# The first tile of a neighbour-maximum kernel is picked before the rest of its batch is prepared

## What is computed

```
scores = where(adj != 0, -arange(N), -inf)
vals, idx = top_k(scores, 25);  valid = vals > -inf
feats = where(valid[..., None], x[idx], -inf);  agg = feats.max(axis=2)
agg = where((degree <= 25)[..., None], maximum(agg, 0), agg)
out = relu(concat([x, agg]) @ W + b)
result = layernorm(x + out)
```

## Time and profile before

| | |
|---|---|
| time, median of 3 runs | 627.07 us (624.03 to 629.14) |
| profiled execution | 624.25 us, of which the span is 622.4 us |
| PE busy | 501.3 us (81%) |
| DVE busy | 534.3 us (86%) |
| ACT busy | 394.6 us (63%) |
| POOL busy | 290.4 us (47%) |

### The profile page before, as it was taken

How to read it: one execution, slowest core, us unless ns; L and a number is a source line. 1 busy time by engine, 2 the same in 40 slices (tenths; PEclk the granted TensorE clock), 3 DMA queues, 4 the chain that set the end, 5 groups by cost and what they waited for, 6 DMA issues and landing times.

```text
span 622.4 us, 14481 instructions
## 1 busy us (share of the span) xinstructions
PE 501.3 (81%) x4480; PEld 341.9 (55%) x4544; DVE 534.3 (86%) x973; ACT 394.6 (63%) x751; POOL 290.4 (47%) x462
## 2 busy tenths in 40 slices
PE   1366997889968996889974999679987999779982
PEld 0124675566654675456752666555764567555762
DVE  4656999899898998899995998998898999998884
ACT  3361577448965688557864588665886478545744
POOL 2643365246633655146733356335552467336610
PEclk9997999899998999799997999998999999899996
DMA  8982336353434647345534445355544463021102
GB/s 244 224 221 72 102 98 129 98 153 96 134 95 137 151 115 125 106 130 143 132 97 112 133 107 137 86 141 137 135 124 120 116 141 59 18 57 36 46 10 70
DMA packets 91815, 71.38 MB, mean 115 GB/s; under 512 B 63651, under 2 KB 80294, under 8 KB 91686
## 3 DMA queue, kind: packets, MB, share of 16 engines
q1 hardware_dynamic: 85286, 56.77, 35.6%
q0 software_dynamic: 6400, 13.12, 8.4%
HBM read 50.99 MB, written 4.19 MB: 89 GB/s over the span
## 4 chain that ended last, share of the span: by engine, by line
PE 30%; DVE 22%; issue 14%; ACT 12%; DVEq 8%; DMA 7%; another core or an unknown queue 3%; POOL 1%; SPq 1%; POOLq 1%; ACTq 0%
PE pair L1037 25%; DVE part L776 11%; DMA adj_sb<-in_adj 3%; ACT row_work L712 3%; DMA g_feat<-in_x,g_idx 3%; DVE hot L771 3%; ACT mask L586 3%; DVEq L846 3%; DVEq L915 2%; ACT distance L629 2%; ACT hot L636 2%; DVE g_feat L849 2%; PE misc L1082 1%; DVE g_val L817 1%
## 5 line engine op out<-in xcount | busy, mean ns | idle before, releaser
L1037 PE MATMUL pair<-hot,x_part 128*128 128x128 bf16 (+3 forms) x3120 | 416.6, 281 | 66.0 <-DVE part L776 33.8
L1037 PEld LDWEIGHTS pair<-hot,x_part 128*128 128x128 bf16 x3120 | 239.0, 99 | 176.1 <-issue 64.0
L776 DVE TENSOR_REDUCE part<-pair 128x128 f32<-128x1024 f32 (+1 forms) x256 | 279.8, 1099 | 47.2 <-PE pair L1037 45.9
L484 POOL DMA_INDIRECT g_feat<-in_x,g_idx x200 | 192.8, 964 | 112.5 <-issue 96.0
L521 POOL TENSOR_TENSOR y_sb<-relu_sb,x_sb 128x128 f32<-128x128 f32 x64 | 32.8, 512 | 194.1 <-ACT relu_sb L647 193.8
L593 ACT ACTIVATE V<-p_V 128x512 bf16<-128x512 f32 x98 | 58.0, 592 | 93.4 <-remote 71.7
L621 ACT ACTIVATE hot<-V,first_bias 128x1024 bf16<-128x1024 bf16 x56 | 64.1, 1145 | 52.8 <-PE pair L1037 52.8
L771 DVE TENSOR_SCALAR hot<-V 128x1024 bf16<-128x1024 bf16 x224 | 84.3, 397 | 0.0
L586 ACT ACTIVATE mask<-adj_sb 128x1024 bf16<-128x1024 uint32 x56 | 58.8, 1050 | 20.5 <-DMA adj_sb<-in_adj 20.5
L636 ACT ACTIVATE hot<-distance,one 128x1024 bf16<-128x1024 bf16 x56 | 64.0, 1143 | 0.2
L629 ACT ACTIVATE distance<-V,second_bias 128x1024 bf16<-128x1024 bf16 x56 | 63.7, 1137 | 0.0
(11 more groups left out here) (88 smaller groups left out, 396.6 us busy)
## 6 DMA issues: line engine op xcount, KB each, us to landing
adj_sb<-in_adj SPq DMA_DIRECT2D x56, 512.0 KB
g_adj<-in_adj SPq DMA_DIRECT2D x8, 512.0 KB, 4.4
x_sb<-in_x SPq DMA_DIRECT2D x8, 512.0 KB, 3.9
out<-y_sb SPq DMA_DIRECT2D x7, 512.0 KB, 5.1
g_feat<-in_x,g_idx POOLq DMA_INDIRECT x200
maskT<-mask SPq DMA_TRANSPOSE x56
out<-y_sb SPq DMA_DIRECT2D x1, 448.0 KB, 3.0
w_sb<-in_W SPq DMA_DIRECT2D x1, 128.0 KB, 6.3
```

Source lines behind the costliest of these rows:

```text
L484: pool.indirect_dma_start(out=g_feat[w][:, k, :], out_offset=None, in_=x_rows, in_offset=bass.IndirectOffsetOnAxis(ap=g_idx[w][:, k:k + 1] ...
L776: dve.tensor_reduce(part[:, par(q, s), :, p], slots_of(q, s, p).rearrange("f k i -> f i k"), AX.X, ALU.max).then_inc(s_used, 1)
L1037: last = pe.matmul(dst, x_part[:, q, part_no, kb], one_hot, start=(first and part_no == 0), stop=(final and part_no == PARTS - 1))
```

## The change

The start prepares only tile 1. In its place the first pass of the loop (batch 0, tile 1) picks its six groups and prepares a tile behind each: tiles 2 to 7, and then tile 1 of batch 1. The level check of batch 0 comes when tile 7 is counted, so behind the sixth group. The features of batch 0 are split earlier and their second and third part come from two whole DVE subtractions in place of sixteen on POOL. Extraction steps 3 to 8 of tile 0 move from the start into the groups of tile 1 and the first of tile 2; the 25 gathers of batch 0 are issued in tiles 3, 4 and 5 as 9, 9 and 7, in place of 5 in each of tiles 1 to 5. On SP the load two tiles on is issued ahead of a tile's transpose, no longer behind it. Batches 1 to 7 are as before, apart from where steps 0 to 2 and 4 to 8 of batch 1's extraction lie in batch 0's tiles.

```diff
+        def to_prepare(i, q, s):
+
+            if is_first(i, q) and s == 1:
+                return [ahead(0, 0, 1, n) for n in range(1, FRONT + 1)]
+            t = ahead(i, q, s, FRONT)
+            return [t] if t else []
...
+                    for t in to_prepare(i, q, s):
+                        to_load, to_turn = ahead(*t, 3), ahead(*t, 1)
+                        if to_load:
+                            sp.wait_ge(s_mask, pos(*to_load) - 1)
+                            load_adj(*to_load)
+                        if to_turn:
+                            transpose_mask(*to_turn)
...
+            transpose_mask(0, 0, 1)
             load_adj(0, 0, 2)
-            load_x(0, 0)
             sp.dma_start(w_sb[:, :, :], W.rearrange("(h f) o -> f h o", h=2)).then_inc(s_const, 16)
             for k in range(PARTS):
                 sp.dma_start(bias[k:k + 1, :], b.rearrange("(a d) -> a d", a=1)).then_inc(s_bias, 16)
-            transpose_mask(0, 0, 1)
-            for n in range(2, FRONT + 3):
-                sp.wait_ge(s_mask, n - 1)
-                load_adj(*ahead(0, 0, 1, n))
-                if n <= FRONT + 1:
-                    transpose_mask(*ahead(0, 0, 1, n - 1))
+            load_adj(0, 0, 3)
+            transpose_mask(0, 0, 2)
+            load_adj(0, 0, 4)
...
             def gather0(i, q, s):
-                if s == 1:
+                first, each = (3, -(-K // 3)) if is_first(i, q) else (1, GATHER)
+                if s == first:
                     wait(s_idx0, 2 * i + q + 1)
                     if not is_first(i, q):
                         wait(s_g0max, 2 * i + q)
-                gather(0, s_g0, range(GATHER * (s - 1), min(GATHER * s, K)))
+                gather(0, s_g0, range(max(each * (s - first), 0), max(min(each * (s - first + 1), K), 0)))
...
-            split_rest(0, 0)
             pool.wait_ge(s_reach, 1)
             reach = reach_tab.rearrange("p j (t b) -> p j t b", b=NT)
             for a, z in ALIKE:
                 for j, slot in enumerate(SHARED[a]):
                     for kb, r in slot:
                         pool.memset(reach[:, j, a - 1:z, kb], float(r)).then_inc(s_reach, 1)
-            split_low(0, 0)
             split_bias()
...
+                    early = is_first(i, q) and s == 1
+                    a = None if early else (to_prepare(i, q, s) + [None])[0]
+                    if early:
+                        for t in to_prepare(i, q, s)[:2]:
+                            copy_V(*t, 0)
+                            copy_V(*t, 1)
+                            make_mask(*ahead(*t, 2))
                     if nxt:
                         first_rank(*nxt)
                         second_distance(*nxt)
...
+                    if early:
+                        t = to_prepare(i, q, s)[2]
+                        copy_V(*t, 0)
+                        copy_V(*t, 1)
+                        make_mask(*ahead(*t, 2))
+                    if a and ahead(*a, 2):
+                        make_mask(*ahead(*a, 2))
...
+                    if early:
+                        for t in to_prepare(i, q, s)[3:]:
+                            copy_V(*t, 0)
+                            copy_V(*t, 1)
+                            make_mask(*ahead(*t, 2))
+                    elif a:
+                        copy_V(*a, 1)
...
+            split_high(0, 0)
             make_mask(0, 0, 2)
-            for n in range(FRONT + 1):
-                if n == FRONT:
-                    act.wait_ge(s_tab, TABLES)
-                    first_rank(0, 0, 1)
-                    second_distance(0, 0, 1)
-                    second_rank(0, 0, 1)
-                if n < FRONT:
-                    make_mask(*ahead(0, 0, 1, n + 2))
-                if n == 0:
-                    split_high(0, 0)
-                if n == 3:
-                    split_mid(0, 0)
+            split_mid(0, 0)
+            act.wait_ge(s_Vp, 1)
+            nc.scalar.activation(V[:, 0, 0, 0:BANK], pairs[1][:, 0:BANK], ACT.Copy).then_inc(s_V, 1)
+            act.wait_ge(s_tab, TABLES)
+            first_rank(0, 0, 1)
+            second_distance(0, 0, 1)
+            second_rank(0, 0, 1)
+            make_mask(0, 0, 3)
...
+            FIRST_EXTRACT = {1: {}, 2: {1: 0, 3: 1}, 3: {1: 2, 3: 3}, 4: {2: 4}, 5: {0: 5, 2: 6}, 6: {}, 7: {1: 7, 2: 8}}
+            FIRST_STEPS = {(1, 0): 3, (1, 1): 4, (1, 2): 5, (1, 3): 6, (1, 4): 7, (2, 0): 8}
...
+                        early = begin and s == 1
+                        if levels_at(i, q, s) and p == (COUNT[s] - 1 if early else 1):
+                            count_violations(i, q, s)
+                            if early:
+                                set_levels(i, q, s)
+                        if p == (COUNT[s] - 1 if levels_at(i, q, s) else 1):
                             lv = load_level(i, q, s)
                         if (s, p) in GATHERED:
                             if GATHERED[s, p][0] == 0:
...
+                        if begin and (s, p) in FIRST_STEPS:
+                            step_written(0, FIRST_STEPS[s, p])
+                            extraction(0, 0, (FIRST_STEPS[s, p],), 0, False)
...
-            dve.memset(viol[:, 0, :, NT + 1:], 0.0)
+            dve.memset(viol[:, :, :, :], 0.0)
             dve.wait_ge(s_falling, 1)
             dve.wait_ge(s_adj0, 16)
-            for st in range(LAST_STEP + 1):
-                if st == LAST_STEP:
-                    dve.wait_ge(s_tab, TABLES)
+            for st in range(3):
                 step_written(0, st)
                 extraction(0, 0, (st,), 0, False)
-                t = st - (LAST_STEP - MT + 1)
-                if t >= 1:
-                    first_V(t)
+            dve.wait_ge(s_high, 1)
+            dve.tensor_tensor(x_rest[:, :, :], x_sb[:, 0], x_part[:, 0, 0], ALU.subtract).then_inc(s_rest, NT)
+            dve.wait_ge(s_Vp, 2)
+            dve.tensor_copy(V[:, 0, 0, BANK:2 * BANK], pairs[1][:, BANK:2 * BANK]).then_inc(s_V, 1)
+            dve.wait_ge(s_mid, 1)
+            dve.tensor_tensor(x_part[:, 0, 2], x_rest[:, :, :], x_part[:, 0, 1], ALU.subtract).then_inc(s_split, NT)
             one_hots(0, 0, 1, range(ACT_RANKS, DEPTHS[1][0]))
-            first_V(MT)
+            dve.wait_ge(s_tab, TABLES)
...
+            def first_tile(i, q, s):
+
+                pe.wait_ge(s_split, NT)
+                for p, t in enumerate(to_prepare(i, q, s)[:MT - 1]):
+                    if p < COUNT[s]:
+                        pick_group(i, q, s, p)
+                    rank_product(*t, 0)
+                    rank_product(*t, 1)
+                    count(*t)
+                    if p == 2:
+                        pe.wait_ge(s_V, 2 * pos(*t) + 2)
+                        turn_features(i, q, TURNS[s])
+                        pe.wait_ge(s_xtc, TURNS[s] + 1)
+                violations(i, q, s)
+                t = ahead(i, q, s, FRONT)
+                rank_product(*t, 0)
+                rank_product(*t, 1)
+                pe.wait_ge(s_level, level_pass(i, q, s))
+                count(*t)
+                pe.nop(nofuse=True)
+                repair(i, q, s, 2 * pos(*t) + 2)
...
             pe.wait_ge(s_tab, TABLES)
             pe.wait_ge(s_tab2, 2)
-            for s in range(1, NT):
-                pe.wait_ge(s_mT[par(0, s)], 16 * nth(0, 0, s))
-                if s > 2:
-                    pe.wait_ge(s_V, 2 * (s - 2))
-                for h in range(2):
-                    pe.matmul(pairs[s % 2][:, BANK * h:BANK * (h + 1)], rank_bf[:, :], maskT[:, par(0, s), h * N // 2:(h + 1) * N // 2],
-                              start=True, stop=True).then_inc(s_Vp, 1)
-                count(0, 0, s)
-            pe.wait_ge(s_const, 16)
-            pe.wait_ge(s_bstep, 9)
+            pe.wait_ge(s_mT[par(0, 1)], 16)
+            for h in range(2):
+                pe.matmul(pairs[1][:, BANK * h:BANK * (h + 1)], rank_bf[:, :], maskT[:, par(0, 1), h * N // 2:(h + 1) * N // 2],
+                          start=True, stop=True).then_inc(s_Vp, 1)
+            count(0, 0, 1)
             run(pe, step)
```

More of the change, by code:

```diff
@@ L929, in step @@
                     nxt = (i, q, s + 1) if s < MT else None if last else (ni, nq, 1)
-                    steps = {} if last else EXTRACT[s]
+                    steps = {} if last else FIRST_EXTRACT[s] if begin else EXTRACT[s]
                     gaps = COUNT[s] - 1
```

120 lines of the change are left out of this document (60 added, 60 removed).

## The result

| | before | changed |
|---|---|---|
| median | 625.55 us (622.15 to 629.14, 4 runs) | 636.78 us (635.96 to 643.01, 4 runs) |
| profiled execution | 624.25 us, span 622.4 us | 636.82 us, span 635.1 us |
| mean granted clock | 0.956 | 0.943 |

The changed kernel takes 1.020 times as long, 95% interval 1.011 to 1.029. It is slower, as forecast: 636.8 us against 635.5 us predicted, inside the range of 628 to 641.5 us. Whether the loss is more than 2% the interval leaves open. Some executions fall into a slower state, with a lower granted clock, and the ratios are formed without them, so that they differ a little from those of the medians.

The account below looks back on a forecast made before the run. Bounds: PE waiting for masks and one-hots, then PE and DVE in step, gathers just in time. 624.25 + 1.05 (tile 2) + 7.4 (gathers) = 632.7 us, 635.5 us on the median's footing; range 628 to 641.5 us.

Parts of the forecast that it names:

- The gathers: Batch 0, tiles 3 to 5: POOL issues the last gather later, DVE waits for it in tile 6; +7.4 us.
- a start that gives back all it wins: First tile: PE picks 18.5 us earlier, but slower preparation of tiles 2 to 7 eats that up.
- Tile 2: Start of tile 2 in batch 0, taken at 62.0 us against 60.95 us before; cost +1.05 us.
- the stretch behind it: From known level to tile 2's start: 9.5 us in place of 10.65, one DVE reduction being done before.
- the half rate through the whole first tile: Rival: PE at half rate in all of tile 1, tile 2 at 66.5 us, gathers late, 640 us; chance 0.12.
- the fast end: First tile with PE at full rate: level known at 50.0 us, tile 2 starts at 59.5 us.
- my half-rate list: First tile at PE's half rate: V of tiles 2 to 7 complete at 23.4, 28.4, 34.7, 41.8, 46.8, 54.3 us.
- The first pick: PE's first pick in tile 1, expected at 19.5 us, 18.5 us earlier than in the kernel before.
- The transposes: Start: a mask's transpose behind a load is usable 4.5 us after issue; V of tiles 6 and 7 waits for it.
- The preparation did not keep its old pace: Denies the rival: preparation at today's pace, tile 2 at 45.3 us, 8.2 us won, 619 us; chance 0.05.
- The gathers do end last: Denies the rival: DVE or PE late anyway, or wait made good in tile 7, 626 to 631 us; chance 0.11.
- The quick start: Rival: transposes usable after 2.8 us, tile 2 at 57.5 or 56.0 us, gathers late, 629.5 to 631 us; chance 0.23.

Follow-up runs that it names:

- the second experiment: Changed kernel with tile 0's extraction one step earlier and batch 0's gathers again five in each of tiles 1 to 5; 626.46 us, ratio 1.0052.
- the mended order and the extra matmuls: Changed kernel with indices early, mask 3 earlier, tile 2's one-hots later, transposes before loads, unread PE matmuls; 678.8, 680.8, 679.91 us, ratios 0.984, 0.989, 0.988.
- the extra matmuls: Changed kernel plus unread PE matmuls, 64 before the first pick and six between the halves of each rank; 632.63 us, ratio 1.0121.

## Why the prediction was right

**The direction and its two causes stand.** Late gathers and a start that gives back all it wins were forecast. The gathers were then taken alone, in the kernel before: 8.8 us. What is left without them is 2.9 us, and the two add up to the whole within their intervals; that the 2.9 us arise in the start is not shown. The closeness of 636.8 to 635.5 us is in part luck. The forecast was 8.45 us more than the kernel before, measured are 11.2 us, and 1.5 us of the difference is hidden by the kernel before, whose median came out at 625.55 us in place of the 627.07 us that I had added to.

**The gathers: +7.4 us predicted, +8.3 us measured.** From tile 2's start to where DVE goes on were 38.48 us before (99.43 less 60.95) and are now 46.79 us (109.93 less 63.14); I had 45.85 us. The first gather comes at +9.29 us (predicted +9.05), the last at +44.05 us (predicted +43.25), since some issues take 1.1 to 1.2 us in place of 0.94 us, and the data follow 2.74 us later in place of 2.54 us. The wait of DVE is 6.85 us; "about 5 to 6 us" was short by the same 0.9 us.

**Tile 2: +1.05 us predicted, +2.2 us measured.** The level was known at 52.56 us, between my 50.0 and 57 us. My 62.0 us puts the level at 52.5 us, a value picked between the two bounds; that it fits so well is luck. The term that was mis-sized is the stretch behind it: I took 9.5 us in place of 10.65 us because DVE's reduction at 51.39 us is done before. Measured are 10.58 us. The rows say why: now `hotx` starts 2.29 us after the level with DVE idle, so that reduction lay beside a wait in the kernel before too and was free. This was readable beforehand, in a row of DVE in the kernel before that I did not use: `hotx` came 2.2 us after the level's end at 50.30 us there as well.

```profile
52.53 1.25 DVE L783 TENSOR_SCALAR hotx<-V 128x128 bf16<-128x128 bf16 x8
```

**PE's clock.** I gave the half rate through the whole first tile 0.12, and it is nearly what came: 512 columns 0.42 us apart up to 37 us, although the granted clock of the window is 1.00. My ground for the fast end, that the clock had held over one gap at 60.95 us, did not carry over to the start. The Trainium skill's rule (TensorE: Matmul & The Clock Gate, "What's actually happening"), that the lower level is the default and activity has to release it, agrees with the matmul spacing, not with the column. But that rival's 66.5 us did not come: V of tiles 2 to 7 was complete at 22.0, 26.5, 32.5, 39.8, 44.3 and 50.3 us, 1.4 to 2.5 us ahead of my half-rate list up to tile 6 and 4 us at tile 7. The first pick was 1.2 us earlier than I worked out (18.26 us for 19.5), and the long fifth group ran at the higher clock at its end. When the clock rises differs between executions: in the second experiment's, after the same idle 2.17 us, the half rank takes 0.39 us at 31.84 us, where the changed kernel's takes 0.61 us at 31.29 us. Three executions of one kernel, that with the mended order and the extra matmuls, differ in the same way: the group of six matmuls of 512 columns at some 22 us takes 1.98, 1.46 and 2.47 us, and tile 2 starts at 56.27, 54.94 and 57.44 us. So of the 3.4 us between the starts of tile 2 of the second experiment and of the changed kernel (59.70 and 63.14 us) part is probably chance.

**The transposes.** I counted 4.5 us from issue to use and let them end last in tiles 6 and 7. At the half rate they ended nothing; at the full rate they did, in tiles 3 and 7, with 5.9 us. Two terms that lean on each other were right only one at a time.

**The rivals.** The preparation did not keep its old pace: tile 7's V came at 50.3 us. The gathers do end last, as the 0.80 us of the earlier trace rows said. The quick start did not come by itself; made by hand, with the extra matmuls and the transpose ahead of the load (one run, in the slower surroundings), a mask was used 2.8 us after its transpose's issue and tile 2 started at 57.59 us, where I had 57.5.

**What remains.** 1.1 us (the stretch behind the level) and 0.9 us (the gathers) are 2 of the 4.1 us by which the profiled execution, 636.82 us, lies above the sum of 632.7 us. The other 2 us come later: at the wait of batch 0 the changed kernel is 10.5 us behind, at that of batch 1 11.07 us (180.97 against 169.90), at the last 13.05 us (608.61 against 595.56), then 12.6 us. The mean granted clock is 0.94 and 0.95 in two stretches of 260 us behind the wait, against 0.95 and 0.96 before. It is more than a difference between two executions: over all runs of the first set the mean granted clock is 0.957 in the kernel before (13 runs) and 0.954 in that with late gathers alone (4), but 0.940 to 0.942 in the three with the new start (4, 10 and 4) and 0.932 in the changed kernel (4). Whether the lower clock makes these kernels slower, and what in the new start brings it about, no run tells; it stays open.

## What to carry to other kernels

An engine that is brought to its first useful work earlier may win nothing if the work that it used to wait through, here the masks, their transposes and the copies, now lies in the same chain: sum that chain at both rates of PE, and mend the queue's order before the clock. And when a pipeline's side work (here 25 serial gathers at 1.25 us) only just meets its deadline, moving its start is the expensive part of a change, however little of the diff it is. A step that ran while its engine would have waited anyway must not be booked as saved, as the reduction behind the level was. And a kernel's early gain is not yet its time: look for it again at the last batch.

## What the runs showed of the hardware that was not expected

- **A transpose in the tail of the gathers.** From the last gather's issue to DVE going on are 2.54 us before and 2.74 us after. In the kernel before with late gathers it is 5.1 us (103.49 to 108.61 us), and there a transpose was issued at 102.81 us; with the extra matmuls 3.9 us (105.93 to 109.85 us), transpose at 105.43 us. In the changed kernel the transpose comes at 108.68 us, behind the last. Where the transpose is issued 2.1 us or more before the last gather, the tail is short (before: 94.80 us and 2.54 us; indices early: 93.42 us and 2.61 us). No run moved the transpose alone.
- **DVE beside POOL.** The one-hot operation at 96.21 us takes 2.98 us; before, such a row is 0.18 us (94.84 us). It ends as POOL's `x_rest` (eight operations, 96.41 to 99.52 us) nears its end, and in the kernel with the extra matmuls the same pair stands at 94.92 us with 2.96 us. The Trainium skill (SBUF — State Buffer, "Who interferes with whom") states that DVE and GpSimd share one port pair as an exclusive lock; the rows agree with it in part. POOL was already at a residual (95.99 us) when this operation began. But in the kernel before a one-hot operation at 90.47 us, in the midst of `x_rest` (88.42 to 91.73 us), takes 0.59 us, where others of its kind take 0.42 us, so such a pair doesn't always cost that much. It cost nothing here, since DVE waits for the gathers afterwards.
- **The same kernel at 624 and at 685 us.** The kernel before took 623.56 us in one set of runs and 685.36 us in the last, on a chip with the same number, so the chip alone does not seem to decide it. In the slower surroundings PE, while POOL issues nine gathers in a row, works in small pieces, as this timeline of the kernel with extra matmuls and SP's order alone shows, and ACT and DVE go on only after the burst. The changed kernel's first trace has no such gap over 0.26 us between 84 and 97 us. Why is not known.

```profile
89.82 0.41 PE L1075 MATMUL pair<-hot,x_part 128*128 128x256 bf16 x2 [0.99 <-issue]
91.38 0.38 PE L1075 MATMUL pair<-hot,x_part 128*128 128x256 bf16 x2 [1.15 <-issue]
92.82 0.43 PE L1075 MATMUL pair<-hot,x_part 128*128 128x256 bf16 x2 [1.06 <-issue]
```
